# A decoder layer on one core: ternary weights worked off in seven batches instead of eight, the last batch's rows loaded and turned in another order, two constants kept once

## The reference, cut to what matters

```
x = x + attention(layernorm(x))          # 32 heads of 64, 8 key/value groups, rope, alibi, 30*tanh(s/30), causal
x = x + longconv(ctx, ctx, layernorm(x)) # per head: outer products of ctx rows, causal convolution of length 256..512, times q
x = x + ffn(layernorm(x))                # silu(gate)*up, rms norm, down
```

## Time and profile before

| | |
|---|---|
| median of 3 runs | 1266.0 us (1265.83 to 1267.7) |
| the profiled execution: own time, span of its instructions | 1264.74 us, 1263.0 us |
| PE busy | 1212.9 us (96%) |
| DVE busy | 940.2 us (74%) |
| ACT busy, POOL busy | 608.6 us (48%), 566.7 us (45%) |
| a middle batch, from the same instruction to the next batch's | about 84.8 us |
| mean granted TensorE clock | 0.995 |

### The profile page before, as it was taken

The page is one execution under the profiler, slowest core; times in us unless marked ns, Lnnn a source line. Parts: engine busy times, 40 slices in busy tenths (PEclk is TensorE's granted clock), DMA queues, the critical chain, the costliest instruction groups (busy, mean ns, idle before and its releaser), DMA issues.

```text
span 1263.0 us, 20179 instructions
## 1 busy us (share of the span) xinstructions
PE 1212.9 (96%) x7330; PEld 828.8 (66%) x7330; DVE 940.2 (74%) x1280; ACT 608.6 (48%) x728; POOL 566.7 (45%) x493
## 2 busy tenths in 40 slices
PE   4988999999999999999999889999999999999998
PEld 3645556657557556576565457777787877877784
DVE  5798878878887788788888888989836545553654
ACT  5785575774765846747647720000134323332331
POOL 1444353543534535436345429999543222322321
PEclk9999999999999999999999989999999999999999
DMA  9463323543435235424345528776000000000000
GB/s 311 128 199 102 113 87 102 153 145 93 127 129 150 82 109 154 153 80 136 117 132 174 184 50 152 150 136 130 1 2 1 18 17 18 0 17 17 1 18 34
DMA packets 128008, 123.80 MB, mean 98 GB/s; under 512 B 31628, under 2 KB 89234, under 8 KB 127954
## 3 DMA queue, kind: packets, MB, share of 16 engines
q1 hardware_dynamic: 103000, 116.86, 30.2%
q10 hardware_dynamic: 24960, 6.29, 3.3%
HBM read 81.63 MB, written 35.21 MB: 93 GB/s over the span
## 4 chain that ended last, share of the span: by engine, by line
PE 78%; DVE 8%; ACT 5%; issue 3%; DMA 3%; POOL 2%; SPq 1%; ACTq 0%; DVEq 0%; POOLq 0%
PE bank L820 12%; PE bank L894 8%; PE bank L895 8%; PE bank L587 8%; PE bank L589 8%; PE bank L588 8%; PE bank L672 6%; PE bank L917 4%; PE bank L916 4%; PE bank L673 3%; PE bank L651 3%; PE bank L650 3%; ACT region_c L1042 1%; DMA unit_halves<-halves 1%; POOL parts L1838 1%
## 5 line engine op out<-in xcount | busy, mean ns | idle before, releaser
L1838 POOL TENSOR_TENSOR parts<-parts 128x512 f32<-128x512 f32 x80 | 130.3, 1633 | 174.2 <-DVE parts L1303 173.9
L587 PE MATMUL bank<-hT_hi,w_hi 128*128 128x256 f16 x640 | 176.1, 275 | 1.0 <-ACT v L978 0.5
L588 PE MATMUL bank<-hT_lo,w_hi 128*128 128x256 f16 x640 | 175.9, 275 | 0.0
L589 PE MATMUL bank<-hT_hi,w_lo 128*128 128x256 f16 x640 | 175.8, 275 | 0.0
L820 PE MATMUL bank<-kv,toep 128*128 128x288 f32 (+2 forms) x660 | 160.1, 405 | 2.3 <-ACT qT L1081 2.2
L1843 POOL TENSOR_SCALAR_AFFINE_SELECT region_c<-region_c 128x512 f32<-128x512 f32 x128 | 103.1, 828 | 122.6 <-ACT region_c L1045 122.6
L820 PEld LDWEIGHTS bank<-kv,toep 128*128 128x128 f32 x660 | 125.0, 192 | 36.8 <-ACT qT L1081 2.8
L672 PE MATMUL bank<-region_c,v 128*128 128x512 f32 x256 | 132.5, 599 | 8.3 <-DVE ctx L1324 8.2
L1042 ACT ACTIVATE region_c<-bank,cap_scale 128x1536 f32<-128x1536 f32 x64 | 98.6, 1541 | 53.0 <-PE bank L651 52.9
L1972 POOL TENSOR_TENSOR sqsum<-sqsum,toep 128x512 f32<-128x512 f32 x56 | 71.2, 1271 | 110.0 <-ACT toep L1214 109.9
L1849 POOL TENSOR_TENSOR ctx_lo<-ctx,ctx_hi 128x512 f16<-128x512 f32 x64 | 74.2, 1160 | 93.8 <-ACT ctx_hi L1020 93.8
(11 more groups left out here) (176 smaller groups left out, 2733.4 us busy)
## 6 DMA issues: line engine op xcount, KB each, us to landing
unit_halves<-halves SPq DMA_DIRECT2D x80, 256.0 KB, 2.2
q_both<-unit_halves SPq DMA_DIRECT2D x64, 256.0 KB, 2.9
wffn<-w_gu SPq DMA_DIRECT2D x8, 1024.0 KB, 5.5
q_high<-unit_halves SPq DMA_DIRECT2D x64, 128.0 KB, 3.0
toep<-kernel_padded SPq DMA_DIRECT2D x32, 256.0 KB, 3.9
cpair<-ctx_pairs SPq DMA_DIRECT2D x32, 176.0 KB, 5.3
xin<-x SPq DMA_DIRECT2D x8, 512.0 KB, 3.5
region_o<-wq SPq DMA_DIRECT2D x4, 1024.0 KB, 11.6
```

What stands on the lines that cost most here:

```text
L587: pe.matmul(dst, lh, rh, start=first and k == 0, stop=False)
L588: pe.matmul(dst, lh, rl, start=False, stop=False)
L589: mm = pe.matmul(dst, ll, rh, start=False, stop=last and k == n - 1)
L1838: pool.tensor_tensor(slot[:, 0], slot[:, 0], slot[:, 1], ALU.add).then_inc(unit_summed, 1)
```

## The change

- The ternary weights are worked off in seven shares (`SHARES` = B - 1) of seven tiles (`WQT` = 7), so each instruction of this work on a full share has 3584 elements a partition instead of 3072. The spreads take three and four tiles instead of three and three. The last batch works off no share, only the end of the seventh. The first share loads 3 tiles of one weight and 4 of the other, and stores 2 and 4.
- In the last batch the 14 tiles of x2 come in two DMAs (6 and 8 tiles), are standardised behind `normalise(4)` to `normalise(7)`, and are turned behind certain outputs and values (the tables `X2_BEHIND_...`), the last of them ahead of `output(7)`. POOL's first two `products` come behind `low_ctx(6)` and `low_ctx(7)`. POOL's third waits until all of x2 is standardised.
- The sine table holds sin once, not -sin and sin; `rotate` reads it twice, and `add_parts` is two POOL instructions of 256 elements, a subtraction and an addition, in place of one of 512.
- The block of ones beside the values is shared by two groups (values, ones, values). `rsumT` now lies behind the scores' buffer, where the longer threshold buffer overlaps it.

The core of the diff:

```diff
-WQT = (2 * HID * D + D * HID) // (P * 512) // B
-GUT = 2 * HID // P // B
+SHARES = B - 1
+WQT = 7
+GUT, FIRST_GUT = 5, 2
+FIRST_PT, PT_OF_BLOCK = 4, 2
+P_BLOCKS = B
...
-            sin_s = sb1("sin_s", [P, 2, S])
+            sin_s = sb1("sin_s", [P, S])
-            v1 = sb1("v1", [P, TT, NG, P])
-            region_c = sb1("region_c", [P, 3 * REP * CAUSAL])
+            v1 = sb1("v1", [P, TT, NG // 2, 3 * DH])
+            region_c = sb1("region_c", [P, 3 * REP * CAUSAL + 2 * S])
-            rsumT = sb1("rsumT", [P, 2 * S])
...
-        X2_AT = {NG: range(0, 3), NG + 1: range(3, 6), STEPS + 5: range(6, 9), STEPS + 6: range(9, 12),
-                 STEPS + 7: range(12, X2_EARLY)}
+        X2_LOADS = (range(0, 6), range(6, X2_EARLY))
+
+        X2_BEHIND_OUTPUT = {3: range(0, 3), 5: range(8, 11), 6: range(11, X2_EARLY)}
+        X2_BEHIND_VALUES = {6: range(3, 5), 7: range(5, 8)}
+        X2_BEHIND_NORMALISE = {4: range(0, 4), 5: range(4, 7), 6: range(7, 9), 7: range(9, X2_EARLY)}
...
             sp.wait_ge(unit_filled, UNITS * B)
-            load_x2(slice(0, (B - 1) * TT))
+            for n in range(2):
+                load_x2(n)
             for h in range(AHEAD):
                 load_head(h, h)
-            store_ffn(B - 1)
...
                 for step in range(STEPS):
                     filler(b, step)
+                    if step == NG:
+                        pe.wait_ge(tanh_done, NG * B)
+                    for n in X2_BEHIND_OUTPUT.get(step - WO_AFTER, ()):
+                        turn_x2(n)
                     if step < NG:
                         scores(b, step)
                     if step >= 2:
                         values(b, step - 2, False)
-                    if step == NG:
-                        pe.wait_ge(tanh_done, NG * B)
-                    for n in X2_AT[step] if step in X2_AT else ():
+                    for n in X2_BEHIND_VALUES.get(step - 2, ()):
                         turn_x2(n)
...
-                    if step == 5:
-                        round_share(b)
-                    if step == 7:
-                        for part in range(2):
-                            spread(b, gthr, w_by, THRESHOLDS, part)
...
-                dve.tensor_tensor(slot[:, 1], src[:, ::-1, :], sin_s[:], ALU.mult).then_inc(unit_turned, 1)
+                dve.tensor_tensor(slot[:, 1], src[:, ::-1, :], sin_s[:].unsqueeze(1).to_broadcast([P, 2, S]), ALU.mult).then_inc(unit_turned, 1)
...
-                    if step == 6:
-                        find_thresholds(b)
-                    if step == 7:
-                        for n in range(4):
-                            standardise_x2(n)
-                    if step == NG:
-                        for n in range(4, 6):
-                            standardise_x2(n)
-                        find_above(b, w_by)
-                    if step == NG + 1:
-                        for n in range(6, 10):
-                            standardise_x2(n)
-                find_below(b, w_by)
-                for n in range(10, X2_EARLY):
-                    standardise_x2(n)
-                scale_digits(b, 0, gscale[:].unsqueeze(3).to_broadcast([P, WQT, 512 // GROUP, GROUP]))
-                scale_digits(b, 1)
+                    for n in X2_BEHIND_NORMALISE.get(step - 2, ()):
+                        standardise_x2(n)
...
-                scale_digits(b, 2)
...
                 pool.wait_ge(unit_turned, UNITS * b + n + 1)
-                pool.tensor_tensor(slot[:, 0], slot[:, 0], slot[:, 1], ALU.add).then_inc(unit_summed, 1)
+                pool.tensor_tensor(slot[:, 0, 0], slot[:, 0, 0], slot[:, 1, 0], ALU.subtract)
+                pool.tensor_tensor(slot[:, 0, 1], slot[:, 0, 1], slot[:, 1, 1], ALU.add).then_inc(unit_summed, 1)
...
-                    if 7 <= step < 9:
-                        pool.wait_ge(toep_in[step - 7], 32)
-                        products(step - 7)
                 for g in range(STEPS - 4, NG):
                     low_ctx(b, g)
+                    pool.wait_ge(toep_in[g + 4 - STEPS], 32)
+                    products(g + 4 - STEPS)
...
+            pool.wait_ge(h2_done, B * TT)
             for n in range(2, AHEAD):
```

More of the change, by code:

```diff
@@ L60 @@
 AHEAD = 4
-WQT = (2 * HID * D + D * HID) // (P * 512) // B
-GUT = 2 * HID // P // B
+SHARES = B - 1
[3 more added lines that the diff above has]
+P_BLOCKS = B
+assert FIRST_GUT + (SHARES - 1) * GUT == 2 * HID // P and FIRST_PT // PT_OF_BLOCK + SHARES - 1 == P_BLOCKS
 LN_EPS = 1e-5
@@ L321, in decoder_layer @@
         quant_stored = sem("quant_stored")
-        x2r_in = sem("x2r_in")
+        x2r_in = [sem(f"x2r_in{n}") for n in range(2)]
         tern_in = sem("tern_in")
@@ L543, in _ @@
                 place_early(b + 1)
+            store_x2(0)
+            late_units(1)
+            store_first_ffn()
+            next_share(1)
+            next_inputs(1)
+            with sp.Fori(2, B - 2) as b:
+                store_x2(b - 1)
+                late_units(b)
+                store_ffn(b - 1)
+                next_share(b)
+                next_inputs(b)
             store_x2(B - 3)
             late_units(B - 2)
+            store_ffn(B - 3)
             next_share(B - 2)
@@ L554, in _, with load_x2 @@
                 place_units(B - 1, range(n, n + 1))
-            def load_x2(tiles):
+            def load_x2(n):
+                tiles = slice(X2_LOADS[n].start, X2_LOADS[n].stop)
                 rows = x2_d[tiles.start * P:tiles.stop * P]
-                sp.dma_start(x2r[:, tiles, :], rows.rearrange("(n p) d -> p n d", p=P)).then_inc(x2r_in, 16)
+                sp.dma_start(x2r[:, tiles, :], rows.rearrange("(n p) d -> p n d", p=P)).then_inc(x2r_in[n], 16)
             sp.wait_ge(unit_filled, UNITS * B)
-            load_x2(slice(0, (B - 1) * TT))
+            for n in range(2):
+                load_x2(n)
             for h in range(AHEAD):
                 load_head(h, h)
-            store_ffn(B - 1)
             with sp.Fori(0, HM // AHEAD - 1) as n:
@@ L736, in last_batch @@
                     output(b, g)
-                    for n in X2_AT[STEPS + g]:
+                    for n in X2_BEHIND_OUTPUT.get(g, ()):
                         turn_x2(n)
@@ L1012, in take_sums @@
                         act.wait_ge(rsum_turned, NG * b + g)
-                    last = act.copy(rsum[o * DH:(o + 1) * DH], bank[DH:P, pv_bank(g, o), :])
+                    last = act.copy(rsum[o * DH:(o + 1) * DH], bank[SUMS[g % 2], pv_bank(g, o), :])
                 last.then_inc(sums_copied, 1)
@@ L1028, in round_share @@
             def round_share(f):
-                act.wait_ge(wffn_in, 32 * (f + 1))
+                act.wait_ge(wffn_in, LOADS * f + FIRST_LOADS)
                 act.copy(w_bf[:], wffn[:]).then_inc(w_rounded, 1)
             def spread(f, what, dst, step, part):
-                rows = slice(part * (WQT // 2), (part + 1) * (WQT // 2))
+                tiles = (slice(0, WQT // 2), slice(WQT // 2, WQT))[part]
                 act.wait_ge(quant_step, QUANT_STEPS * f + step)
-                act.copy(dst[:, rows].rearrange("p t (n c) -> p t n c", c=GROUP),
-                         what[:, rows].unsqueeze(3).to_broadcast([P, WQT // 2, 512 // GROUP, GROUP])
+                act.copy(dst[:, tiles].rearrange("p t (n c) -> p t n c", c=GROUP),
+                         what[:, tiles].unsqueeze(3).to_broadcast([P, tiles.stop - tiles.start, 512 // GROUP, GROUP])
                          ).then_inc(spread_done, 1)
@@ L1091, in last_batch @@
                         take_values(b, step)
+                    for n in X2_BEHIND_OUTPUT.get(step - WO_AFTER, ()):
+                        take_x2(n)
                     if step >= 2:
@@ L1323, in normalise @@
                     rows = slice(o * DH, (o + 1) * DH)
[L1324 removed]
+                    dve.tensor_tensor(ctx32[rows, g % 2].rearrange("p h s -> p (h s)"), bank[OWN[g % 2], pv_bank(g, o), :],
                                       rsumT[rows], ALU.mult).then_inc(pv_free, 1)
@@ L1495, in standardise_x2 @@
                 if n == 0:
-                    dve.wait_ge(x2r_in, 16)
                     dve.wait_ge(rstd_done, B + 1)
+                for part, tiles in enumerate(X2_LOADS):
+                    if n == tiles.start:
+                        dve.wait_ge(x2r_in[part], 16)
                 if n == X2_EARLY:
```

109 lines of the change are left out of this document (62 added, 47 removed).

## The result

The changed kernel took 1263.1 us (median of 18 runs, 1260.6 to 1264.8) beside 1265.2 for the kernel before on the same chips (18 runs, 1263.3 to 1268.3): a ratio of 0.9982, 95% interval 0.9974 to 0.9989. The profiled execution took 1261.7, its span 1259.8. I had forecast 1268.0. The kernel moved by two per mille, and the other way.

The account below looks back on a forecast made before the run. PE, busy 96% of the span, was taken to bound the kernel. 9.8 + 2.0 + 2.9 - 0.9 - 9.5 - 2.3 = +2.0 on the profiled 1264.74 gave 1266.7, 1268.0 for the median; range 1259 to 1272.

Parts of the forecast that it names:

- No rival: Four alternative outcomes for the whole kernel: 1260.5 (chance 0.25), 1270.3 (0.18), 1274.8 (0.12) and 1256.5 (0.05).
- The period of a middle batch: Start of batches 2 to 6: each 1.95 longer, five such starts, +9.8, the largest term.
- The unit's sum is 2.1 late ... so they come 1.95 later: Middle batch start: POOL's second half waits for find_above; ACT's cast, soften(0), take_values(0) and PE's project come 1.95 later.
- The lower bound, 0.8 a batch: Middle batches: if POOL's second half slips in ahead of DVE, only the sizes count, 0.8 a batch, +4.0.
- Batch 0 and the start of batch 1: Longer ternary work ahead of a tanh PE waits for, plus the split adds: +2.0, between 1.5 and 3.
- The split adds lie on the chain several times in batch 0, at 0.1 to 0.28 each: Batch 0: split sums lengthen the chain; with a sine table half as long set against them, +0.5, between 0 and 1.5.
- The terms of the ternary work, +1.5: Batch 0: find_thresholds +0.56 and four spreads +0.95, directly ahead of the tanh PE waits for.
- forecast 2.9: Last batch's start: 1.33 late at low_unit plus longer DVE instructions of +1.61, ahead of rotate of unit 7.
- -0.9 and -9.5: Last batch: smaller waits for rows from DRAM in its middle, -0.9; DVE's ternary work gone at its end, -9.5.
- so 10.6 us: Last batch, 706 to 748.2: PE's idle time of 10.6 is what the change can win.
- Rival 3: Last batch's end wins 5 in place of 9.5, with the clock falling: +6.8, 1274.8; chance 0.12.
- If the two waits go, the clock should hold: Start of the full convolution: without the waits the granted clock doesn't fall to half, -2.3; if it falls anyway, 0.

Follow-up runs that it names:

- experiment 1: before_split_sums: kernel before with the sine kept once and each unit's sum made by two POOL instructions; 1272.8, ratio 1.0054.
- experiment 2: Changed kernel with each unit's sum in one POOL instruction of 512 elements, the first halves' subtraction left out; 1257.4, ratio 0.9941.
- experiment 9: Changed kernel with ACT's cast of unit 6 behind the next soften(0) and take_values(0), DVE's low_unit of unit 6 moved too; 1255.2, ratio 0.9924.
- experiment 10: Kernel of experiment 9 with scale_digits part 1 moved from step 2 to step 5 in batches 1 to 6; 1251.2, ratio 0.9892.
- experiment 7: before_first_split: kernel before with only batch 0's unit sums made in two halves, the sine still stored twice; 1264.1, ratio 1.0001.
- Experiment 4: Kernel before without the last batch's ternary share, so an eighth of the ternary weight is left out; 1255.5, ratio 0.9924.
- experiment 3: after_old_turns: changed kernel with the last batch's tiles standardised and turned at the old steps, two loads and seven shares kept; 1266.9, ratio 1.0010.
- experiment 8: Changed kernel with the last batch's rows loaded in one DMA in place of two; 1264.8, ratio 1.0002.
- before_again: The kernel before run once more, unchanged, for the granted clock at the start of the full convolution; 1262.8, a single run.
- experiment 6: after_unit_first: changed kernel with low_unit of unit 6 ahead of find_above in DVE's queue, batches 1 to 6; 1262.0, ratio 0.9982.
- experiment 5: Changed kernel with find_above of batches 1 to 6 in four instructions, three of them behind low_unit of units 2 to 4; 1262.7, ratio 0.9985.

## Why the prediction was wrong

The sum was +2.0 where -3.2 was measured: three terms were each about 1.9 too high, all in the same direction. In the middle batches and the last one the mechanisms were there and a size was off; in batch 0 the split had the wrong sign. No rival took place.

**The period of a middle batch: mis-sized, 1.57 instead of 1.95.** The step "The unit's sum is 2.1 late ... so they come 1.95 later" had the order right (experiments 1, 2 and 9 show order, engine and queue). Its size failed in two places. `find_above` stands for the rest of the first half, 0.52 (2.55 recorded, 2.03 alone), not for 0.69, and `soften(0)` comes 1.68 later and not 1.95. Of that PE had margin: its waits at the start are 0.87 and 0.52 in a middle batch, and one of 0.38 later shrinks to 0.25. That is 1.26 of idle time, and 0.28 of busy time comes to it, which goes with the number of waits (see the last batch): a batch with one such wait has PE busy for 84.42 and 84.45 (before, experiment 10), with two 84.67 (experiment 2), with three 84.69 and 84.70 (experiment 1, after). The Trainium skill ("SBUF — State Buffer", "Who interferes with whom") has the later of two such instructions wait for the whole of the other; the trace agrees in 2.50 recorded for a half that takes 0.73 undisturbed. The lower bound, 0.8 a batch where only the sizes count, was near: experiment 2 measured 0.52.

**Batch 0 and the start of batch 1: wrong in sign for the split.** "The split adds lie on the chain several times in batch 0, at 0.1 to 0.28 each" counted the longer pair and not that DVE waits for a shorter piece. The same exclusion that costs 1.5 in a middle batch gives 0.95 over five units here (experiment 7). The terms of the ternary work, +1.5, measured 1.12 (from `find_thresholds(0)` to `find_above(0)`, 10.35 before, 11.47 after). The rest of the +0.1 is 0.34 at the start of batch 1 and 0.4 that lies within what batch 0 varies.

**The last batch: right in kind, too little given.** The start took 2.6 more up to PE's wait of 1.50 for the context at 684.56, forecast 2.9. From there to the full convolution it was -12.1, where -0.9 and -9.5 had been written, 1.7 too little. Windows over just these stretches show of what kind it is, the kernel before first, then the one after:

```profile
674.00:748.12 74.12, 62.61 (x287) 0.98 0.40 129
```

```profile
684.56:746.62 62.06, 59.94 (x287) 1.00 0.42 137
```

PE's idle time fell by 9.4, from 11.5 to 2.1. Ahead of 706 that was 0.4, where 0.9 had been written, and behind it 9.0, where 8.7 had been (the 9.5 without the 0.8 of the clock; the sum takes 1.0 for a wait that the text beside it puts at 1.6, and 0.38 was measured). So the idle part came out right. The same 287 instructions were also recorded 2.7 shorter, and of this only 0.8 had been written, for transposes at the slow clock. The clock's share is 0.46: the eight transposes take 1.73 at 745.44, and 1.27 in before_first_split, in the same place behind the same wait at a clock of 1.00.

The other 2.2 goes with the waits, and here a step failed: "so 10.6 us" and "That is what the change can win" take PE's recorded idle time for the whole of what the waits cost. Transposes in a row without a wait show what is missing, two rows of the kernel before and one of the kernel after:

```profile
728.72 0.60 PE L720 MATMUL bank<-ident_s,hbuf 128*128 128x128 f32 x4
719.18 1.47 PE L720 MATMUL bank<-ident_s,hbuf 128*128 128x128 f32 x12
```

```profile
719.42 1.04 PE L768 MATMUL bank<-ident_s,hbuf 128*128 128x128 f32 x8
```

Each further one adds 0.11, but a single one is recorded with 0.27. The last one ahead of a wait therefore counts as busy for 0.16 more than one with another behind it, and the second one behind a wait starts 0.17 after the first, not 0.11. The kernel before has 13 waits in its window, the kernel after 4. Counted from start to start over all of PE's records there, and without the share of the clock, the instructions just ahead of a wait take 2.1 longer than others of their kind before and 0.6 after, those just behind one 0.6 and 0.15: 1.9 of the 2.2. The rest is in pieces under 0.2.

Experiment 4, with neither the longer instructions nor the split, gains 7.3 from `find_above(6)` to the full convolution by the removed work alone; the kernel after gains 9.4 there, its start of 2.6 already taken off. Without the new steps it loses 3.3 again, without the second load 2.75 (experiments 3 and 8); the two need not add, since early steps are of use only if the rows are there. Rival 3, that the end doesn't get what it is given, is refuted by these windows.

**The clock: the size right in this pair of profiles, the reason not established.** 2.2 was measured for 2.3. But the step "If the two waits go, the clock should hold" treats the fall as a property of the order of turns. With that order and the ternary work beside it, it fell at the start of the full convolution in three of four profiled executions (before, before_split_sums, before_again) and held there in one (before_first_split) with the same waits. In the nine other kernels, which don't have the wait of 2.0 there, it held there each time. It did not hold everywhere in them: four of them (experiments 2, 6, 9 and 10) wait 2.18 to 3.49 at the start of the last batch, and in each the granted clock was 0.50 for 3.4, from the end of that wait or up to 1.2 behind it. Experiment 2's wait, and its window a little later:

```profile
679.32 1.12 PE L720 MATMUL bank<-region_c,v 128*128 128x512 f32 x2 [2.18 <-DVE ctx L1371]
```

```profile
681.00:683.00 2.00, 2.00 (x11) 1.41 (x10) 1.70 (x5) 1.99 (x3) 0.00 (x0) 0.50 0.44 131
```

The other five, which wait 1.50 or less there, show no fall. So at these two places a wait of 2.0 or more went along with a fall in seven of eight cases, and the eighth shows that the wait alone doesn't decide it. How much of the median's difference is the clock's stays open.

The three terms at their measured sizes take 5.8 off the sum of +2.0, the ffn puts 0.5 and the clock 0.1 on it: -3.2 on 1264.7, near the 1261.7 of the profiled execution. The range of 1259 to 1272 held the time, but the forecast of 1268.0 was 4.9 too high and on the wrong side of the kernel before.

## What to carry to other kernels

An instruction cut in two changes who waits for whom: the other engine gets in between. Here that gained 0.95 where DVE's own way set the pace (experiment 7, though no difference in the time could be told) and lost 1.5 a batch where the second half released something. So look at each meeting by itself and give it its sign. And before moving the instruction that collides, look at what is queued behind its victim: here the collision could stay as it was, and moving a 0.6 us cast behind the next tanh, with the instruction that reads it, brought the time from 1263.1 to 1255.2, while cutting the colliding instruction into pieces gave nothing. Two costs in one batch need not add (1.55 and 0.52 gave 1.57); measure them apart and together. And PE's recorded idle time is less than what its waits cost: here 9 waits fewer gave 2.2 us beyond the idle time.

## What the runs showed of the hardware

- Four DVE instructions with the work of one were recorded at 4.59 us together beside POOL's half sums, the one at 2.55 (experiment 5).
- Two POOL half sums of 256 elements that nothing disturbs are recorded at 0.73 each and start 0.69 apart, so about 1.4 for the pair.
- 128x128 f32 transposes in a row start 0.11 apart; a single one is recorded with 0.27. A wait of PE costs this difference beside its recorded idle time.
- The granted clock at the start of the full convolution differed between executions with the same instructions and the same waits ahead (0.50 and 1.00 in the window of 748 to 750). At the start of the last batch it was 0.50 for 3.4 us in the four kernels in which PE waited 2.18 to 3.49 there, and 1.00 where it waited 1.50.
- Batch 0, in which the weights come in, ended up to 2.5 us apart in executions of the same instructions: `find_thresholds(0)` at 133.74 (after_unit_first) and 136.28 (after_old_turns), which are the same program up to there. The cause was not looked for. A single profile is no measure of a term of 1 us there.
